# Attention, one turn in another order on all engines: six runs of score units for eight, the shared bank used twice in one turn, stack fills in the first turns

## The chip, the cores and the metric

The kernel runs on one core of a Trainium2 chip. The core has TensorE (PE in the profile; its weight loads are PEld), VectorE (DVE), ScalarE (ACT), GpSimd (POOL) and SyncE (SP), which here issues DMAs. The metric is the device time of one execution in microseconds (us), lower is better. Kernels are compared by the median of their runs.

## What is computed

Two transformer layers on x of 32 samples x 256 tokens x 128 features, in float32: a retention layer, a mixture of 16 experts, a full attention layer, and a layer that routes the best tokens of every sample. The change lies in the third, the attention:

```python
h = layernorm(x)
q = (h @ Wq.T + bq).reshape(b, s, 16, 8) * 8 ** -0.5     # b 32, s 256, 16 heads of 8
k = (h @ Wk.T + bk).reshape(b, s, 16, 8)
v = (h @ Wv.T + bv).reshape(b, s, 16, 8)
scores = einsum('bqhd,bkhd->bhqk', q, k)
out = einsum('bhqk,bkhd->bqhd', softmax(scores), v).reshape(b, s, 128)
x = x + out @ Wo.T + bo
```

## The kernel before, in words

Four phases run one after the other with a barrier between them. `attention_phase` goes through the 32 samples in a software pipeline. On each engine a list of steps with a lag is written out by hand, `pipeline(engine, [(step, lag), ...], B, B)`: in turn `it` (0, 1, 2, ...) the engine issues every step of the list in its order, each for sample `it - lag` where there is such a sample. So a list fixes the order of instructions on its engine, and a lag says how many turns after a sample's first step the step comes. The turns of two engines are tied together by semaphores alone: an instruction waits until what it reads is written and what it overwrites is read.

The steps of one sample, in the order of its data:

- `add_given` (GpSimd) adds the experts' result to x; `stats_of` and `moments` (VectorE), `inv_std` (GpSimd) and `norm` (ScalarE) make the layer norm. For samples 0 and 1 `moments_early` and `inv_std_early` stand at their own places.
- `transpose_h` (TensorE), `copy_hT` (ScalarE), `project_qk` and `project_v` (TensorE), `copy_qk` and `copy_v` (ScalarE).
- `split_qk(0)` and `split_qk(1)` (GpSimd) split k and q into a high and a low part; `store_k` and `store_q` (SyncE) write them to DRAM, and `fill_k` and `fill_q` read them back in another layout into `k_stack` and `q_stack`, which have three buffers. The stacks are set to 1.0 (k, by GpSimd) and 0.0 (q, by VectorE) once, before their first use; that takes three memsets each.
- The scores are made twice, in 8 units each of 4 matmuls (`scores`, L1511). A unit of kind "m" (`for_maximum(j)`, m0 to m7 below) has queries on the partitions, and VectorE reduces it over the keys (`maximum(j)`, L1374). `split_max` (GpSimd), `transpose_max` (TensorE), `copy_maxT` (ScalarE) and `give_max` (SyncE, two small DMAs for each half of the heads) put the maxima into rows of `q_stack`. A unit of kind "e" (`for_exponential(j)`, e0 to e7) has keys on the partitions and subtracts the maximum in the same matmul; ScalarE takes its exponential (`exponential(j)`, L1463), and `values(0)` to `values(3)` (TensorE, L1544) multiply two of them each with v. e0 waits for the maxima of half 0, e4 for those of half 1.
- `copy_o`, `by_token` (called "token" here), `normalise`, `transpose_o`, `copy_oT`, `output`, `add_y` end the attention of a sample; `stats3_of`, `moments3`, `inv_std3`, `norm3`, `weigh`, `add_up` and `store_out` prepare the next phase.

Units go into three PSUM slots of two banks; the table `UNITS` gives for each unit, in TensorE's order, kind, number, lag and slot, and before a unit TensorE waits until the unit that last had its slot has been read (`free_slot`). All else that goes through PSUM for a short time (v, oT, y, max0, max1, hT, token, qk) takes turns in one bank, `ps_misc`: `TURNS` lists the users in order, and each waits until the one before it has been read (`misc_free`). A score unit uses TensorE as two tiles of 64 rows, `values` as four tiles of 32 columns, and all other matmuls the whole array.

TensorE's list before has score units in eight runs, that is, with nothing else between them: m7 e7; m0; e0 m1; e1 m2; e2 m3 e3; m4; m5 e4 m6; e5 e6.

## Time and profile before

| | us |
|---|---|
| median of 3 runs (lowest to highest) | 1029.46 (1027.74 to 1031.27) |
| the profiled execution, its own time | 1028.35 |
| its span in the trace | 1026.6 |
| TensorE busy in the span | 909.6 (89%) |
| VectorE, ScalarE, GpSimd busy | 712.4, 637.1, 607.9 |

The time of an execution and its span differ by 1.75 us, which lies around the program. In the view of 40 slices attention takes slices 17 to 36. The chain that ended last covers only a tenth of the span and names the last phase alone, since each phase ends at a barrier; so what bounds attention has to be read from its own stretch: the busy time of the engines there, and the timeline of one turn. In a timeline a matmul's duration includes what it overlaps with the next, so lengths on TensorE are taken from start to start.

### The profile page before, as it was taken

How to read it: one execution, taken by the hardware profiler on the slowest of the kernel's cores; microseconds unless marked ns; L12 is line 12 of the kernel's file. 1: busy time of each engine (PE TensorE's matmuls, PEld its weight loads, DVE VectorE, ACT ScalarE, POOL GpSimd, SP SyncE). 2: the span in 40 equal slices, each digit the busy share in tenths (PEclk: the TensorE clock that was granted, in tenths of full speed). 3: DMA queues.
4: the chain of work that ended last, by engine and by line, in shares of the span. 5: the costliest groups of instructions: out<-in, count | busy, mean ns of one | idle time of the engine just before them, and what ended most of it. 6: DMA issues, size and time to landing. Idle time of an engine off the chain costs nothing. (4 is left out here: it accounts for less than half of the span.)

```text
span 1026.6 us, 28744 instructions
## 1 busy us (share of the span) xinstructions
PE 909.6 (89%) x10129; PEld 683.6 (67%) x10130; DVE 712.4 (69%) x1551; ACT 637.1 (62%) x1304; POOL 607.9 (59%) x1277
## 2 busy tenths in 40 slices
PE   6999999499989999169999999999999999944766
PEld 5888888279989999145666666666666666523654
DVE  4888888575544454347788888888888888826652
ACT  4777776322224444127888888888888888743552
POOL 4777776267737767544566676666676665344003
PEclk9999999699999999558999999999999999986998
DMA  8700000221123332134343545443444333202000
GB/s 310 294 3 2 3 2 2 80 76 54 50 69 95 91 92 78 59 124 146 115 146 111 152 127 157 127 130 124 134 147 137 120 123 116 68 17 68 3 3 21
DMA packets 66773, 96.88 MB, mean 94 GB/s; under 512 B 10706, under 2 KB 57426, under 8 KB 62162
## 3 DMA queue, kind: packets, MB, share of 16 engines
q1 hardware_dynamic: 61394, 84.00, 26.0%
q0 software_dynamic: 5248, 11.15, 3.2%
q8 instruction: 80, 1.31, 0.5%
q14 instruction: 51, 0.42, 0.1%
HBM read 57.60 MB, written 36.47 MB: 92 GB/s over the span
## 5 line engine op out<-in xcount | busy, mean ns | idle before, releaser
L1374 DVE TENSOR_REDUCE a_neg_max<-a_slot 128x4 f32<-128x1024 f32 x256 | 306.0, 1218 | 83.5 <-PE a_slot L1511 66.3
L1463 ACT ACTIVATE a_pT<-a_slot 128x1024 f32<-128x1024 f32 x256 | 255.5, 1026 | 8.9 <-PE a_slot L1511 5.2
L1544 PE MATMUL a_ps_o<-a_pT,a_v_pad 128*32 128x256 f32 x2048 | 137.9, 387 | 0.0
L1511 PE MATMUL a_slot<-a_k_stack,a_q_stack 62*128 62x256 f32 x1024 | 120.6, 316 | 4.2 <-DMA a_q_stack<-q_dram 2.4
L1511 PE MATMUL a_slot<-a_q_stack,a_k_stack 64*128 64x256 f32 x1024 | 114.5, 312 | 3.7 <-ACT a_pT L1463 1.9
L1511 PEld LDWEIGHTS a_slot<-a_k_stack,a_q_stack 62*128 62x128 f32 x1024 | 79.5, 191 | 46.7 <-issue 22.2
L727 POOL DMA_INDIRECT y_rows<-m_total,m_token x80 | 81.2, 1015 | 45.9 <-issue 32.9
L1511 PEld LDWEIGHTS a_slot<-a_q_stack,a_k_stack 64*128 64x128 f32 x1024 | 75.5, 187 | 34.9 <-issue 23.4
L331 DVE TENSOR_TENSOR r_score<-ps_score,r_decay 128x512 f32<-128x512 f32 x128 | 81.5, 678 | 7.9 <-PE ps_score L490 7.8
L1544 PEld LDWEIGHTS a_ps_o<-a_pT,a_v_pad 128*32 128x32 f32 x2048 | 53.6, 109 | 45.8 <-issue 19.4
L968 PE MATMUL m_banks<-m_xeT,m_w_pair 128*128 128x128 f32 x640 | 79.6, 278 | 0.0
L720 POOL DMA_INDIRECT sorted_in<-h,m_slot x64 | 63.9, 998 | 26.1 <-issue 18.6
L968 PEld LDWEIGHTS m_banks<-m_xeT,m_w_pair 128*128 128x128 f32 x640 | 76.1, 195 | 0.3 <-ACT m_xeT L878 0.3
L849 DVE COPY m_w_pair<-expert_up 128x512 f32 x80 | 31.2, 432 | 57.9 <-PE m_banks L968 57.3
L386 ACT ACTIVATE r_h<-x,r_shift,r_rstd 128x128 f32<-128x128 f32 x128 | 56.7, 497 | 12.2 <-POOL r_shift L258 11.7
L920 PE MATMUL m_banks<-h2T,shared_up 128*128 (+1 forms) x256 | 61.6, 385 | 2.5 <-DVE m_hidden L776 2.4
L870 ACT ACTIVATE m_gate<-m_banks 128x512 f32<-128x512 f32 x32 | 19.1, 597 | 66.7 <-PE m_banks L920 66.7
L885 ACT ACTIVATE m_gate_e<-m_banks 128x512 f32<-128x512 f32 x40 | 23.9, 597 | 57.6 <-PE m_banks L968 57.6
L1277 POOL TENSOR_TENSOR a_max_part<-a_neg_max,a_zeros 128x16 fp32r<-128x16 f32 x64 | 13.6, 212 | 70.6 <-DVE a_neg_max L1374 68.2
L1306 POOL TENSOR_TENSOR a_v_pad<-a_v_tok,a_zeros 128x128 f32<-128x128 f32 x64 | 24.2, 399 | 52.4 <-PE a_ps_o L1544 52.4
L920 PEld LDWEIGHTS m_banks<-h2T,shared_up 128*128 128x128 f32 x256 | 47.0, 193 | 9.0 <-issue 3.7
L1279 POOL TENSOR_TENSOR a_part<-a_qk,a_part 128x256 fp32r<-128x256 f32 x64 | 46.6, 727 | 5.0
(290 smaller groups left out, 2027.1 us busy)
## 6 DMA issues: line engine op xcount, KB each, us to landing
a_k_stack<-k_dram SPq DMA_DIRECT2D x64, 256.0 KB, 3.0
a_q_stack<-q_dram SPq DMA_DIRECT2D x64, 256.0 KB, 3.5
k_dram<-a_part SPq DMA_DIRECT2D x64, 128.0 KB
q_dram<-a_part SPq DMA_DIRECT2D x32, 256.0 KB
sorted_in<-h SPq DMA_DIRECT2D x10, 528.0 KB, 13.3
m_xe<-sorted_in SPq DMA_DIRECT2D x40, 132.0 KB
expert_up<-in_eu_dram SPq DMA_DIRECT2D x1, 4096.0 KB, 24.8
out_dram<-e_x_plus_h SPq DMA_DIRECT2D x32, 128.0 KB, 2.1
```

The source lines that it names most:

```text
L331: nc.vector.tensor_tensor(score[:, p, tile], ps_score[tile][:], own, ALU.mult).then_inc(score_done, 1)
L386: ins = nc.scalar.activation(h[:, p, t], x_sb[:, s * TPS + t, :], ACT.Identity, bias=shift[:, p, t:t + 1], scale=rstd[:, p, t:t + 1])
L720: nc.gpsimd.indirect_dma_start(sorted_in, bass.IndirectOffsetOnAxis(ap=slot[:, t:t + 1], axis=0), h2_all[:, t, :], None).then_inc(scattere ...
L727: nc.gpsimd.indirect_dma_start(y_rows, bass.IndirectOffsetOnAxis(ap=token[:, at:at + 1], axis=0), ye[:, t % RING, j], None).then_inc(store ...
L849: ins = nc.vector.tensor_copy(w_pair[:, p % 2, j], w_up[:, dve_experts[t][j]])
L920: ins = nc.tensor.matmul(bank[2 * which + p][:, f * S:(f + 1) * S], shared_up[:, which, f], h2T_all[:, bass.ds(s * S, S)], start=True, sto ...
L968: ins = nc.tensor.matmul(bank[PAIR * (p % 2) + j][:, f * P:(f + 1) * P], w_pair[:, p % 2, j, f * P:(f + 1) * P], xeT[:, p % 2, j], start=T ...
L1279: nc.gpsimd.tensor_tensor(low.bitcast(F32R), value, high, ALU.subtract).then_inc(steps, 1)
L1374: nc.vector.tensor_reduce(neg_max[:, p, half, t, :, g], slots[SLOT_OF["m", j]][:].rearrange("p (c r) s -> p c r s", c=TILES), AX.X, ALU.ma ...
L1463: nc.scalar.activation(pT[:, j % PT_RING], slots[SLOT_OF["e", j]][:], ACT.Exp).then_inc(e_read, 1)
L1511: ins = nc.tensor.matmul(slot[:, tile * UT + r], weights[at, n, half, g * UT + r, of_weights].bitcast(F32R), moving[at, n, half, g * UT + ...
L1544: ins = nc.tensor.matmul(ps_o[q * APAD:(q + 1) * APAD, g // 2], v_pad[:, p, t, g * UNIT + q], pT[:, (2 * g + t) % PT_RING, q], start=g % 2 ...
```

## The change

No arithmetic changes; every engine has the same instructions, in another order, with these differences in the code:

- TensorE's list and `UNITS`: m0 moves to the end of the list with lag 2, so that it stands directly ahead of e0 m1; m4 stands directly ahead of m5 e4; the 16 units stand in six runs, m0 e0 m1; m2 e1; e2 m3 e3; m4 m5 e4; e5 m6 e6; e7 m7. The slots are dealt out anew.
- `project_v` (lag 1 for 2) and `transpose_o` (lag 5 for 6) stand next to each other and share one turn of `ps_misc`: v in the first half of the bank, oT in the second (`MISC_SIDES`). `copy_v` waits in addition until the transposes that share its turn are done.
- The lists of ScalarE, VectorE, GpSimd and SyncE get another order and other lags.
- The memsets of the stacks move from ahead of the first turn into turns 3 to 5 on GpSimd (`preset_k_stack`) and 2 to 4 on VectorE (`preset_q_stack`).

On TensorE in the middle of the phase, `k_stack,q_stack` is a unit of kind m and `q_stack,k_stack` one of kind e, with its slot. Before, from v (L1601) over m7 e7, values(2), m0, oT (L1609), e0 m1, y (L1617) to e1 m2:

```order
L1601 MATMUL a_ps_misc<-a_wv,a_hT 128x128 x2
L1511 MATMUL a_slot0<-a_k_stack,a_q_stack 128x256 x4
L1511 MATMUL a_slot1<-a_q_stack,a_k_stack 128x256 x4
L1544 MATMUL a_ps_o<-a_pT,a_v_pad 32x256 x8
L1511 MATMUL a_slot2<-a_k_stack,a_q_stack 128x256 x4
L1609 MATMUL a_ps_misc<-ident,a_o_tok 128x128 x2
L1511 MATMUL a_slot1<-a_q_stack,a_k_stack 128x256 x4
L1511 MATMUL a_slot0<-a_k_stack,a_q_stack 128x256 x4
L1617 MATMUL a_ps_misc<-a_wo,a_oT 128x128 x2
L1511 MATMUL a_slot2<-a_q_stack,a_k_stack 128x256 x4
L1511 MATMUL a_slot1<-a_k_stack,a_q_stack 128x256 x4
```

m0 stands alone here, between values(2) and oT, and so does m4 later in the turn. Now, where the lines are v L1617, oT L1625, y L1633, values L1555:

```order
L1617 MATMUL a_ps_misc<-a_wv,a_hT 128x128 x2
L1625 MATMUL a_ps_misc<-ident,a_o_tok 128x128 x2
L1522 MATMUL a_slot1<-a_q_stack,a_k_stack 128x256 x4
L1522 MATMUL a_slot0<-a_k_stack,a_q_stack 128x256 x4
L1555 MATMUL a_ps_o<-a_pT,a_v_pad 32x256 x8
L1522 MATMUL a_slot2<-a_k_stack,a_q_stack 128x256 x4
L1522 MATMUL a_slot1<-a_q_stack,a_k_stack 128x256 x4
L1522 MATMUL a_slot0<-a_k_stack,a_q_stack 128x256 x4
L1633 MATMUL a_ps_misc<-a_wo,a_oT 128x128 x2
L1522 MATMUL a_slot1<-a_k_stack,a_q_stack 128x256 x4
L1522 MATMUL a_slot2<-a_q_stack,a_k_stack 128x256 x4
L1593 MATMUL a_ps_misc<-ident,a_max_part 16x128 x2
```

m0 has moved from between values(2) and oT to ahead of e0, and oT from there to directly behind v.

SyncE's queue in the middle of the phase, one turn, before:

```order
L1184 DMA a_k_stack<-k_dram 32x2048 x2
L1202 DMA a_q_stack<-a_max_T 2x4x256 x2
L1193 DMA a_q_stack<-q_dram 32x1x2048 x2
L1202 DMA a_q_stack<-a_max_T 2x4x256 x2
L1171 DMA k_dram<-a_part 16x8x256 x2
L1176 DMA q_dram<-a_part 128x2x256
L1211 DMA out_dram<-e_x_plus_h 128x2x128
```

Here each pair of transfers of maxima has a read back ahead of it. Now:

```order
L1196 DMA a_q_stack<-q_dram 32x1x2048 x2
L1205 DMA a_q_stack<-a_max_T 2x4x256 x2
L1187 DMA a_k_stack<-k_dram 32x2048 x2
L1205 DMA a_q_stack<-a_max_T 2x4x256 x2
L1174 DMA k_dram<-a_part 16x8x256 x2
L1179 DMA q_dram<-a_part 128x2x256
L1214 DMA out_dram<-e_x_plus_h 128x2x128
```

The read back of q stands ahead of both transfers of maxima and of the read back of k, and the stores of the next sample end the turn.

GpSimd at the start of the phase, before (`x<-x,h` is `add_given`, the four small ones `inv_std_early`):

```order
L1230 MEMSET a_k_stack 128x2048 x3
L1237 TENSOR_TENSOR x<-x,h 128x256 x2
L1251 TENSOR_TENSOR a_ve<-a_mv,a_eps 128x2
L1253 TENSOR_TENSOR a_minus_mean<-a_zeros,a_mv 128x2
L1257 TENSOR_TENSOR a_rstd<-a_ve,a_half_pow 128x2
L1259 TENSOR_TENSOR a_shift<-a_minus_mean,a_rstd 128x2
L1237 TENSOR_TENSOR x<-x,h 128x256
```

Here all three memsets stand ahead of the first addition. Now, up to the second memset:

```order
L1242 TENSOR_TENSOR x<-x,h 128x256 x2
L1256 TENSOR_TENSOR a_ve<-a_mv,a_eps 128x2
L1258 TENSOR_TENSOR a_minus_mean<-a_zeros,a_mv 128x2
L1262 TENSOR_TENSOR a_rstd<-a_ve,a_half_pow 128x2
L1264 TENSOR_TENSOR a_shift<-a_minus_mean,a_rstd 128x2
L1235 MEMSET a_k_stack 128x2048
L1242 TENSOR_TENSOR x<-x,h 128x256
L1256 TENSOR_TENSOR a_ve<-a_mv,a_eps 128x2
L1258 TENSOR_TENSOR a_minus_mean<-a_zeros,a_mv 128x2
L1262 TENSOR_TENSOR a_rstd<-a_ve,a_half_pow 128x2
L1264 TENSOR_TENSOR a_shift<-a_minus_mean,a_rstd 128x2
L1235 MEMSET a_k_stack 128x2048
```

The first two additions and the first layer norm stand ahead of the first memset; two memsets still stand ahead of the first `split_qk`, which comes behind the last row and one more `add_given`.

```diff
-UNITS = (("e", 6, 5, 2), ("m", 7, 4, 0), ("e", 7, 5, 1), ("m", 0, 3, 2), ("e", 0, 4, 1), ("m", 1, 3, 0),
...
+UNITS = (("e", 0, 4, 1), ("m", 1, 3, 0), ("m", 2, 3, 1), ("e", 1, 4, 2), ("e", 2, 4, 0), ("m", 3, 3, 2), ("e", 3, 4, 1),
+         ("m", 4, 3, 2), ("m", 5, 3, 0), ("e", 4, 4, 1), ("e", 5, 4, 1), ("m", 6, 3, 0), ("e", 6, 4, 2), ("e", 7, 4, 1),
+         ("m", 7, 3, 0), ("m", 0, 2, 2))
+MISC_SIDES = {"v": (0,), "oT": (1,), "y": (0,), "max1": (0,),
+              "hT": (0,), "token": (0, 1), "qk": (0, 1), "max0": (0,)}
...
+        misc = {name: ps_misc[:, sides[0] * S:(sides[-1] + 1) * S] for name, sides in MISC_SIDES.items()}
...
-            pipeline(sp, [(store_k, 3), (store_q, 3), (store_out, 9), (fill_k, 3), (give_max(1), 5), (fill_q, 3), (give_max(0), 4),
+            pipeline(sp, [(fill_q, 4), (give_max(1), 6), (fill_k, 4), (give_max(0), 5), (store_k, 3), (store_q, 3), (store_out, 10),
...
-            for n in range(BUFS):
-                nc.gpsimd.memset(k_stack[:, n], 1.0).then_inc(preset_k, 1)
+
+            def preset_k_stack(s, p, r):
+                if s < BUFS:
+                    nc.gpsimd.memset(k_stack[:, s], 1.0).then_inc(preset_k, 1)
...
-            pipeline(pool, [(split_max(0), 5), (weigh, 9), (add_given, 0), (inv_std_early, 1), (split_qk(0), 3), (inv_std, 2),
-                            (split_max(1), 5), (split_qk(1), 3), (bias, 5), (pad_v, 4), (inv_std3, 8)], B, B)
+            pipeline(pool, [(weigh, 12), (pad_v, 7), (add_given, 2), (inv_std_early, 3), (split_qk(0), 5), (split_qk(1), 5),
+                            (inv_std3, 10), (split_max(1), 7), (bias, 6), (split_max(0), 6), (inv_std, 3), (preset_k_stack, 3)], B, B)
...
-            pipeline(dve, [(given_added, 0), (maximum(0), 4), (add_up, 9), (add_y, 7), (maximum(1), 4),
-                           (maximum(2), 4), (moments3, 8), (stats_of, 0), (y_is_added, 7), (maximum(3), 4),
-                           (normalise, 6), (maximum(4), 4), (moments, 1), (stats3_of, 7), (maximum(5), 4),
-                           (settle3, 7), (maximum(6), 4), (settle, 0), (moments_early, 0), (maximum(7), 4),
-                           (preset_v_pad, 2)], B, B)
+            pipeline(dve, [(stats_of, 1), (settle_early, 1), (moments_early, 1), (maximum(6), 5), (settle3, 8), (moments3, 8),
+                           (add_up, 10), (settle, 1), (moments, 1), (maximum(7), 5), (maximum(0), 4), (add_y, 7),
+                           (maximum(1), 4), (maximum(2), 4), (y_is_added, 7), (stats3_of, 7), (maximum(3), 4),
+                           (normalise, 6), (maximum(4), 4), (maximum(5), 4), (given_added, 0), (preset_q_stack, 2),
+                           (preset_v_pad, 3)], B, B)
...
             def copy_v(s, p, r):
                 after(act, v_done, s + 1)
+                after_most(act, oT_done, s - 4 + 1, B)
...
-            pipeline(act, [(copy_qk, 1), (exponential(4), 4), (copy_maxT(0), 3), (copy_o(0), 4),
-                           (exponential(5), 4), (exponential(6), 4), (copy_v, 1), (exponential(7), 4),
-                           (copy_oT, 5), (exponential(0), 3), (norm, 0), (copy_maxT(1), 3), (exponential(1), 3),
-                           (copy_o(1), 4), (copy_hT, 0), (exponential(2), 3), (exponential(3), 3),
-                           (norm3, 6)], B, B)
+            pipeline(act, [(copy_maxT(0), 3), (exponential(5), 4), (exponential(6), 4), (exponential(7), 4), (copy_oT, 5), (copy_v, 1),
+                           (exponential(0), 3), (norm, 0), (exponential(1), 3), (copy_maxT(1), 3), (copy_hT, 0),
+                           (copy_o(1), 4), (exponential(2), 3), (exponential(3), 3), (norm3, 7), (exponential(4), 3),
+                           (copy_qk, 0), (copy_o(0), 3)], B, B)
...
-            TURNS = (("v", 2, v_copied, 1, 0), ("oT", 6, oT_copied, 1, 0), ("y", 6, y_added, 1, 0),
...
+            TURNS = ((("y", 6, y_added, 1, 0),), (("max1", 4, maxT_copied, 2, 1),), (("hT", 1, hT_copied, 1, 0),),
+                     (("token", 5, otok_copied, 1, 0),), (("qk", 1, qk_copied, 1, 0),), (("max0", 3, maxT_copied, 2, 0),),
+                     (("v", 1, v_copied, 1, 0), ("oT", 5, oT_copied, 1, 0),))
...
-            pipeline(pe, [(for_exponential(6), 5), (project_v, 2), (for_maximum(7), 4), (for_exponential(7), 5),
-                          (values(2), 5), (for_maximum(0), 3), (transpose_o, 6), (for_exponential(0), 4),
-                          (for_maximum(1), 3), (output, 6), (for_exponential(1), 4), (for_maximum(2), 3),
...
+            pipeline(pe, [(for_exponential(0), 4), (for_maximum(1), 3), (output, 6), (for_maximum(2), 3), (for_exponential(1), 4),
                           (transpose_max(1), 4), (values(3), 5), (transpose_h, 1), (for_exponential(2), 4),
-                          (for_maximum(3), 3), (for_exponential(3), 4), (by_token, 5), (values(0), 4),
...
+                          (for_maximum(3), 3), (for_exponential(3), 4), (by_token, 5), (values(0), 4), (for_maximum(4), 3),
+                          (for_maximum(5), 3), (for_exponential(4), 4), (project_qk, 1), (values(1), 4),
+                          (transpose_max(0), 3), (for_exponential(5), 4), (for_maximum(6), 3), (for_exponential(6), 4),
+                          (project_v, 1), (transpose_o, 5), (for_exponential(7), 4), (for_maximum(7), 3), (values(2), 4),
+                          (for_maximum(0), 2)], B, B)
```

## Rows read from the trace of the kernel before

**Rows 1.** The page of the profile, its first line.
```profile
span 1026.6 us, 28744 instructions
```

**Rows 2.** Stretches: us; busy (count) of PE, PEld, DVE, ACT, POOL; PEclk; DMA, GB/s.
```profile
450.50:470.00 19.50, 17.20 (x96) 11.06 (x96) 14.86 (x18) 7.24 (x13) 8.45 (x22) 0.50 0.46 154
...
491.17:883.09 391.92, 387.88 (x4250) 246.63 (x4246) 328.87 (x547) 337.13 (x581) 256.16 (x598) 1.00 0.43 132
```

**Rows 3.** Timeline, TensorE: start, duration, engine, line, operation; m0, samples 3 and 31.
```profile
491.17 0.50 PE L1511 MATMUL a_slot<-a_k_stack,a_q_stack 62*128 62x256 f32 x4
...
883.09 0.50 PE L1511 MATMUL a_slot<-a_k_stack,a_q_stack 62*128 62x256 f32 x4
```

**Rows 4.** Timeline, TensorE, parts of one turn.
```profile
645.25 0.51 PE L1511 MATMUL a_slot<-a_k_stack,a_q_stack 62*128 62x256 f32 x4
645.68 0.44 PE L1609 MATMUL a_ps_misc<-ident,a_o_tok 128*128 128x128 f32 x2
646.06 0.51 PE L1511 MATMUL a_slot<-a_q_stack,a_k_stack 64*128 64x256 f32 x4
...
649.80 0.50 PE L1511 MATMUL a_slot<-a_q_stack,a_k_stack 64*128 64x256 f32 x4
650.14 0.40 PE L1511 MATMUL a_slot<-a_k_stack,a_q_stack 62*128 62x256 f32 x4
650.38 0.41 PE L1511 MATMUL a_slot<-a_q_stack,a_k_stack 64*128 64x256 f32 x4
650.73 0.66 PE L1588 MATMUL a_ps_misc<-ident,a_oT_pad 128*128 128x128 f32 x4
651.31 1.07 PE L1544 MATMUL a_ps_o<-a_pT,a_v_pad 128*32 128x256 f32 x16
...
654.38 0.40 PE L1511 MATMUL a_slot<-a_k_stack,a_q_stack 62*128 62x256 f32 x4
654.89 0.38 PE L1577 MATMUL a_ps_misc<-ident,a_max_part 128*16 128x128 f32 x2
```

**Rows 5.** Timeline, ScalarE, the same turn.
```profile
646.60 1.03 ACT L1463 ACTIVATE a_pT<-a_slot 128x1024 f32<-128x1024 f32 x1
...
654.29 0.47 ACT L1448 ACTIVATE a_qk<-a_ps_misc,a_bk 128x256 f32<-128x256 f32 x1
```

**Rows 6.** Timeline, SyncE's queue and TensorE; in brackets idle time and its releaser.
```profile
873.63 1.16 SPq L1184 DMA_DIRECT2D a_k_stack<-k_dram  x2
874.83 1.44 SPq L1202 DMA_DIRECT2D a_q_stack<-a_max_T  x2
...
877.75 0.50 PE L1511 MATMUL a_slot<-a_q_stack,a_k_stack 64*128 64x256 f32 x4 [0.56 <-DMA a_q_stack<-a_max_T]
```

**Rows 7.** Timeline of the first turns, GpSimd, VectorE, SyncE's queue, TensorE.
```profile
426.08 5.29 POOL L1230 MEMSET a_k_stack<- 128x2048 f32 x3
...
430.64 1.76 DVE L1329 MEMSET a_q_stack<- 128x2048 f32 x1 [0.38 <-issue]
...
433.37 0.20 POOL L1251 TENSOR_TENSOR a_ve<-a_mv,a_eps 128x2 f32<-128x2 f32 x1 [0.63 <-DVE a_mv L1358]
...
434.75 0.73 POOL L1237 TENSOR_TENSOR x<-x,h 128x256 f32<-128x256 f32 x1
...
440.07 0.61 POOL L1277 TENSOR_TENSOR a_part<-a_qk,a_zeros 128x256 fp32r<-128x256 f32 x1 [2.55 <-ACT a_qk L1448]
...
445.88 1.21 SPq L1193 DMA_DIRECT2D a_q_stack<-q_dram  x2
...
450.50 1.65 PE L1511 MATMUL a_slot<-a_k_stack,a_q_stack 62*128 62x256 f32 x12 [2.44 <-DMA a_q_stack<-q_dram]
```

**Rows 8.** Timeline of the last turns, VectorE.
```profile
915.08 0.45 DVE L1401 BATCH_NORM_STATS2 e_stats<-x 128x6 f32<-128x128 f32 x2
...
918.45 0.42 DVE L1413 TENSOR_REDUCE w_tok<-e_product 128x2 f32<-128x256 f32 x1 [2.92 <-POOL e_product L1317]
918.79 0.24 DVE L1408 BATCH_NORM_AGGREGATE e_mv<-e_stats 128x2 f32<-128x6 f32 x2
```

More of the change, by code:

```diff
@@ L1454, in step @@
                         after(act, max_in[(s - 1) % BUFS][half], 16 * TILES * ((s - 1) // BUFS + 1))
-                    nc.scalar.copy(max_T[:, half], ps_misc[0:PARTS * HH, 0:S]).then_inc(maxT_copied, 1)
+                    nc.scalar.copy(max_T[:, half], misc[f"max{half}"][0:PARTS * HH]).then_inc(maxT_copied, 1)
                 return step
@@ L1548, in values @@
                 return step
[L1551 to L1553 removed]
+            TURNS = ((("y", 6, y_added, 1, 0),), (("max1", 4, maxT_copied, 2, 1),), (("hT", 1, hT_copied, 1, 0),),
+                     (("token", 5, otok_copied, 1, 0),), (("qk", 1, qk_copied, 1, 0),), (("max0", 3, maxT_copied, 2, 0),),
+                     (("v", 1, v_copied, 1, 0), ("oT", 5, oT_copied, 1, 0),))
             def misc_free(name, s):
[L1556 to L1562 removed]
+                at = [name in [user[0] for user in turn] for turn in TURNS].index(True)
+                lags = {user[0]: user[1] for user in TURNS[at]}
+                it = s + lags[name]
+                first = TURNS[at][0][0]
+                if name != first and 0 <= it - lags[first] < B:
+                    return
+                for back in range(1, 4 * len(TURNS)):
+                    it_then = it - (back - at + len(TURNS) - 1) // len(TURNS)
+                    users = [user for user in TURNS[(at - back) % len(TURNS)] if 0 <= it_then - user[1] < B]
+                    for _, lag, read, per, which in users:
+                        after(pe, read, per * (it_then - lag) + which + 1)
+                    if users:
                         return
```

39 lines of the change are left out of this document (15 added, 24 removed).

## The prediction

> **What bounds the kernel now.** I read the stretches first, then the list of TensorE from one unit to the next. m0 of sample 3 starts at 491.17 and m0 of sample 31 at 883.09 [rows 3]: 28 turns in 391.92 us, 14.00 each. In them TensorE is busy for 387.88 us, 99%, at a granted clock of 1.00 (2.4 GHz); ScalarE is busy for 337, VectorE for 329, GpSimd for 256 [rows 2], which is 12.0, 11.7 and 9.1 us a turn. So in these 28 turns, 38% of the span [rows 1], a turn lasts as long as TensorE's list, and a shorter list shortens it until another engine, some 2 us behind, has a wait that TensorE sees. Before 491 the pipeline fills, after 883 it drains; there nothing is full, and chains through all engines count.
>
> A busy share doesn't say whether the list could be shorter; starts do. In the run e2 m3 e3 the units start at 649.80, 650.14 and 650.38, and the next group at 650.73 [rows 4]: 0.34, 0.24 and 0.35 us. A unit in the middle of a run costs 0.24. m0, alone in its run, takes from 645.25 to 645.68, 0.43. So each run costs about 0.19 us beside its units, however many they are. Whole-array groups behave alike: the two transposes of o take 0.38 (645.68 to 646.06), the four of token 0.58 (650.73 to 651.31), so two more in an open group cost 0.20, and opening one 0.18.
>
> **The change, TensorE's list.** The 16 units and all other groups stay; three openings go.
> - Six runs for eight, m0 and m4 no longer alone: 2 x 0.19 = -0.38 us a turn.
> - v and oT next to each other: -0.18. No row shows two different whole-array groups side by side with different operands; the bounds are 0 and -0.20, and I take the value of the token group, the nearest thing.
> - max0 starts 0.51 after m6 (654.38 to 654.89), where the group behind e3 starts after 0.35: its turn in the shared bank has to wait for ScalarE's second activation of qk, which ends at 654.76 [rows 5]. Now a group of values, 1.07 long [rows 4], lies between qk and max0, and the wait goes: -0.10 (0 to -0.16).
>
> Sum: -0.66, a list of 13.34 us.
>
> **Waits that the new order makes.** I lay the other engines beside this list, from m0 = 0: e0 at 0.34, m1 at 0.58, y at 0.91, m2 at 1.55, max1 at 2.3, hT at 3.6, e4 at about 7.1. A slot is free for its next unit at least 0.2 us early for 15 of the 16 units. The exception is m2: it takes the slot of e0, with only m1 and y in between. e0 ends at 0.58, its exponential takes 1.03 [rows 5], so the slot is free at about 1.7 and m2 waits 0.15; e1, max1 and all the rest queue behind it. From there the chain runs e1, its exponential, the copy of max1 (behind it on ScalarE), hT: another 0.05. Together +0.2 (0 to 0.4). A turn then lasts 13.54, 0.46 less; over 28 turns -12.9 us. Bounds: all savings and no wait, -0.66 x 28 = -18.5; the two runs alone and the waits at 0.2, -0.18 x 28 = -5.0.
>
> The added wait in `copy_v` (for the transposes of o) stands on ScalarE ahead of e0's exponential, which TensorE's m2 needs. v and oT end at about 11.7 of the turn, while ScalarE reaches the two copies only behind e7's exponential, near 13.0: it costs nothing as long as ScalarE is that late; if it were earlier it would wait with nothing urgent behind it.
>
> **SyncE's queue.** The maxima of half 1 now go out behind `fill_q`, and e4 waits for them. Their copy ends near 3.8 and e4 is due near 7.3 with the waits above: 3.5 us. From the issue of such a pair right behind `fill_k` (873.63, then 874.83) to the matmul that waited for it (877.75) it took 2.9 us [rows 6]: 0.6 in hand. `fill_q` itself waits for the store of q, which GpSimd's split ends at about the start of the turn, and has to be issued (1.21 us [rows 7]) by 3.8: that is close, and is the rival below. The first `fill_q` needed 4.6 us from its issue (445.88) to the matmul that waited for it (450.50) [rows 7]. The Trainium skill (DMA: Bandwidth & Descriptors, Queues, rings and completion order) says that each DMA engine consumes descriptors in ring order; by that the maxima would land only behind the whole `fill_q`, 4.6 - 1.2 = 3.4 us after their own issue, an estimate. No run here shows the two in this order; the sum would be the same, with 0.1 us in hand for 0.6.
>
> **The start.** GpSimd's three memsets take 5.29 us from 426.08, and only then x is added [rows 7]. The first `split_qk` starts at 440.07, and from it follow the store, the read back and m0 of sample 0 at 450.50. In the new order GpSimd does two additions (0.70 each), waits for the moments, does `inv_std_early` (1.4: 433.37 to 434.75), a memset (1.76, as on VectorE), an addition, `inv_std_early`, a memset, an addition: VectorE had the moments 0.97 after its last memset (430.64 + 1.76, then 433.37); without memsets it can start at about 426.9, behind the bias matmul, so I take 428.0 for the moments, and 428.0 + 2 x (1.4 + 1.76 + 0.7) = 435.7. The split waits for ScalarE's copy of qk as well, which came 5.3 after `inv_std_early` (434.75 to 440.07): now 429.4 + 5.3 = 434.7, earlier. So the first split starts at 435.7, 4.3 us sooner, not 5.3, since two of the three memsets still lie ahead of it. VectorE's memsets (1.76 each) move behind the first moments and are done long before `fill_q`. `fill_q` now goes first and waits for the later store; about even. I take -4.3 for the fill (-2 to -6: in 450 to 470 TensorE runs at 0.50, 1.2 GHz [rows 2], and when it rises isn't set by the order alone; all of that stretch at full clock would be worth some 8 us, a rise a few us later costs half of those).
>
> **The end.** The last sample's `stats3_of` is at 915.08, yet its `moments3` only at 918.79, behind `add_up` of the sample before at 918.45 [rows 8]: in VectorE's list `add_up` of an older sample stands ahead. In the new list `add_up` comes two turns later than `moments3`, and on GpSimd `weigh` of the sample before comes behind `inv_std3` of the last. The last moments can start at 915.6: -3.2 us (0 to -3.3).
>
> Sum: -12.9 - 4.3 - 3.2 = -20.4. The profiled execution took 1028.35, which gives 1008.0; the median of the runs lies 1.1 above it, so 1009. By the bounds: -27.8 to -7.0, that is 1002 to 1022.
>
> **Rivals.**
> - *Another engine becomes the bound.* ScalarE is busy 12.0 us of what would be 13.5, in fixed order, with VectorE at 11.7. If its copies (ahead of hT, token, max0) come late by 0.25 us more, a turn lasts 13.8: -5.6 - 7.5 = -13.1, 1016.
> - *The change doesn't shorten the list*: what a run costs is not in its opening, and returns at other borders. Turns stay at 14.0 and the two ends alone bring -7.5: 1022. Against it stand the two lengths of a unit, 0.43 and 0.24.
> - *Slower: the maxima come late.* The place is `fill_q` ahead of `give_max(1)`. If the store of q lands late, `fill_q` holds SyncE's queue, the maxima go out late, and e4 and all behind it wait in every turn, us for us. The 0.6 in hand go first; a turn is back at 14.0 when they are 1.06 late, and the kernel is slower when the waits also eat the 7.5 of the ends (0.27 a turn), that is from 1.33 on. Two us late gives 13.54 + 1.4 = 14.9: +26 - 7.5, 1048. For it: GpSimd's list, 9.1 us long, starts each turn's chain with a wait for VectorE's m3 and ends it with the split of q. Against: a late e4 delays the next m3 too, from which that chain starts, so part of a delay is paid back.
>
> **How the numbers follow.** My forecast (1002 to 1013) has a chance of 0.58, another engine 0.16, a list that isn't shorter 0.12, late maxima 0.14. About 0.3%, 3 us, is what a measurement of this kernel can tell from no change. Faster by more: the first two, and 0.08 of the third (the ends have to bring over 3 us), 0.82. Slower by more: 0.10 of the late maxima. Between: 0.04 of each of the last two, 0.08. The range is that of the bounds, 1002 to 1022; it leaves out the late maxima and half of the third case, 0.2.
>
> **What would show it.** Right: PE from m0 to m0 near 13.5 us; m5 starting 0.34 after m4; oT about 0.65 behind the start of v and 0.2 long; a small wait at m2 for ScalarE; the first split near 435.7; the last moments right behind the last stats. Wrong: waits at e4 or e0 for the maxima, a turn of 13.8 with idle time ahead of hT or token, or m0 of sample 0 later than 448.

## The result and the profile after

The changed kernel takes 1025.88 us (median of 15 runs, 1022.93 to 1029.41) and the kernel before 1031.27 (15 runs, 1027.74 to 1033.88). The ratio is 0.9948, 95% interval 0.9934 to 0.9962: some 5.4 us faster. The forecast was 1009 with a range of 1002 to 1022, so the sign was right and the size wrong by a factor of four: -20.4 forecast, -5.4 measured. The profiled execution of the changed kernel took 1027.74 (span 1026.0), 1.9 above its median; that of before, 1028.35, lies 2.9 below the median of its 15 runs. So the two traces differ by 0.6 only, and the other 4.8 us lie between profiled executions and medians.

One cut through both traces serves for all that follows: GpSimd's first instruction in attention, the starts of y (`output`) of sample 0, of sample 27 and of sample 31 (y(0), y(27), y(31) below), and the start of the routed layer behind attention. Columns of the order of time: start, time, engine, line, operation, out<-in, count, idle time before. Before:

```profile
425.86 0.10 POOL L1225 MEMSET a_half_pow<- 128x2 f32 x1 [7.84 <-POOLq L97]
...
492.65 0.60 PE L1617 MATMUL a_ps_misc<-a_wo,a_oT 128*128 128x128 f32 x3
870.88 0.71 PE L1617 MATMUL a_ps_misc<-a_wo,a_oT 128*128 128x128 f32 x4
913.60 0.88 PE L1617 MATMUL a_ps_misc<-a_wo,a_oT 128*128 128x128 f32 x4 [0.55 <-ACT a_oT L1476]
926.07 0.59 PE L2162 MATMUL d_ps<-ident,w_tok 128*32 128x128 f32 x2 [11.59 <-PEq L97]
```

After:

```profile
426.71 0.10 POOL L1228 MEMSET a_half_pow<- 128x2 f32 x1 [7.84 <-POOLq L97]
...
492.71 0.71 PE L1633 MATMUL a_ps_misc<-a_wo,a_oT 128*128 128x128 f32 x4
872.96 0.71 PE L1633 MATMUL a_ps_misc<-a_wo,a_oT 128*128 128x128 f32 x4
913.85 0.68 PE L1633 MATMUL a_ps_misc<-a_wo,a_oT 128*128 128x128 f32 x4 [0.55 <-ACT a_oT L1488]
923.42 0.59 PE L2177 MATMUL d_ps<-ident,w_tok 128*32 128x128 f32 x2 [8.88 <-PEq L97]
```

| stage of the trace, us | before | after | change | forecast |
|---|---|---|---|---|
| up to the start of attention | 425.86 | 426.71 | +0.85 | 0 |
| start of attention to y(0) | 66.79 | 66.00 | -0.79 | -4.3 |
| 27 turns, y(0) to y(27) | 378.23 | 380.25 | +2.02 | -12.4 |
| y(27) to y(31), pipeline running empty | 42.72 | 40.89 | -1.83 | -0.5 |
| y(31) to the routed layer | 12.47 | 9.57 | -2.90 | -3.2 |
| routed layer to the end | 100.53 | 102.58 | +2.05 | 0 |
| span | 1026.6 | 1026.0 | -0.6 | -20.4 |

The phases ahead of attention and the routed layer behind it hold code that isn't touched; in all twelve traces attention starts between 425.29 and 426.82. Without those two stages the traces differ by 3.5 us, nearer to the 5.4 of the medians.

The 27 turns hold two things that must be kept apart. By the starts of y, 17 of them last 13.75 to 13.79 us, where before all lasted 14.00 to 14.02: the list did get shorter, by 0.25 a turn, 6.8 us in all. The other ten are longer: 27 x 13.755 is 371.4, and 380.25 were taken, 8.9 more. The longest, from y of sample 19 to that of sample 20, takes 17.42. The stretch that answers to [rows 2] (columns: stretch, length, busy time and count of PE, PEld, DVE, ACT, POOL, then PE's granted clock, DMA share, GB/s) has TensorE busy for 374.64 of 391.20 us, 96% and no longer 99%:

```profile
491.80:883.00 391.20, 374.64 (x4226) 240.10 (x4222) 330.95 (x543) 338.95 (x577) 249.38 (x592) 1.00 0.44 132
```

**A turn without disturbance.** TensorE, one undisturbed turn of after, the places that the forecast spoke of (`k_stack,q_stack` is a unit m, `q_stack,k_stack` a unit e):

```profile
645.31 0.40 PE L1522 MATMUL a_slot<-a_q_stack,a_k_stack 64*128 64x256 f32 x4
...
645.88 0.71 PE L1633 MATMUL a_ps_misc<-a_wo,a_oT 128*128 128x128 f32 x4
646.83 0.51 PE L1522 MATMUL a_slot<-a_k_stack,a_q_stack 62*128 62x256 f32 x4 [0.24 <-ACT a_pT L1475]
647.82 1.07 PE L1555 MATMUL a_ps_o<-a_pT,a_v_pad 128*32 128x256 f32 x16
649.02 0.41 PE L1585 MATMUL a_ps_misc<-ident,a_h 128*128 128x128 f32 x2
...
656.14 0.71 PE L1617 MATMUL a_ps_misc<-a_wv,a_hT 128*128 128x128 f32 x4
656.69 0.38 PE L1625 MATMUL a_ps_misc<-ident,a_o_tok 128*128 128x128 f32 x2
657.00 0.50 PE L1522 MATMUL a_slot<-a_q_stack,a_k_stack 64*128 64x256 f32 x4
```

and ScalarE at the same place:

```profile
645.75 1.02 ACT L1475 ACTIVATE a_pT<-a_slot 128x1024 f32<-128x1024 f32 x1 [0.33 <-PE a_slot L1522]
...
647.61 1.02 ACT L1475 ACTIVATE a_pT<-a_slot 128x1024 f32<-128x1024 f32 x1
648.53 0.35 ACT L1467 COPY a_max_T<-a_ps_misc 16x256 f32<-16x256 f32 x1
```

v and oT together take 0.86 (656.14 to 657.00). y took 0.64 up to the next unit before (646.73 to 647.37); now m2 starts 0.95 behind it, a wait of 0.31: e0 is at its end only at 645.71 (0.40 after its start), its exponential runs from 645.75 to 646.77, and then its slot is free. hT starts 1.20 behind the start of the values group, where another of the same turn is followed after 1.00 (651.86, behind 650.86): 0.20 of waiting for the copy of max1 (648.53 to 648.88), which stands behind e1's exponential.

**The late maxima.** From the waits between 500 and 872 (who waited for whom, us in total, times, the longest): SyncE for landings before, then SyncE and TensorE after:

```profile
SPq L47 <- DMA k_dram<-a_part: 0.3, 1, 0.3
```

```profile
SPq L47 <- DMA q_dram<-a_part: 34.6, 26, 3.6
...
PE a_slot L1522 <- DMA a_q_stack<-a_max_T: 5.0, 7, 2.0
```

Before, SyncE had next to no wait for a landing. After, it waits in 26 turns for the store of q to land, 1.3 us on average and up to 3.6. The longest turn shows what comes of it, on SyncE and TensorE in the order of time, and in the granted clock of two stretches:

```profile
757.95 0.54 SPq L1179 DMA_DIRECT2D q_dram<-a_part  x1
...
762.66 1.20 SPq L1196 DMA_DIRECT2D a_q_stack<-q_dram  x2
763.91 1.42 SPq L1205 DMA_DIRECT2D a_q_stack<-a_max_T  x2
...
764.71 0.74 PE L1522 MATMUL a_slot<-a_k_stack,a_q_stack 62*128 62x256 f32 x8
767.39 0.50 PE L1522 MATMUL a_slot<-a_q_stack,a_k_stack 64*128 64x256 f32 x4 [1.95 <-DMA a_q_stack<-a_max_T]
...
769.28 1.93 PE L1555 MATMUL a_ps_o<-a_pT,a_v_pad 128*32 128x256 f32 x16
```

```profile
764.00:767.00 3.00, 1.44 (x24) 0.74 (x16) 2.66 (x5) 1.56 (x3) 2.47 (x8) 1.00 0.78 216
769.00:771.00 2.00, 2.00 (x17) 0.59 (x16) 0.00 (x0) 0.84 (x2) 0.62 (x2) 0.50 0.00 0
```

Here the store of q is issued at 757.95, `fill_q` only at 762.66, and the maxima of half 1 behind it at 763.91, 2.2 us later in the turn than in an undisturbed one (5.19 behind y for 3.03). e4, which could have followed m5, waits 1.95. Then the granted clock falls to 0.50 (1.2 GHz), and the next values group takes 1.93 for 1.07: with the wait of 1.95 the turn is 3.66 longer than an undisturbed one.

The ten long turns don't have one cause. In five the maxima went out later than 3.03 behind y: in y(19) since the store of q landed 4.65 us after its issue, where the others took 2.3 to 3.1; in y(15) and y(3) since that store was itself issued 1.4 and 0.3 later, in y(15) behind a store of k whose issue took 2.02 for 0.6; in y(10) and y(22) since the issue of `fill_q`'s second transfer took 1.72 and 1.61 for 0.59. In the other five they went out on time and landed late. Their landing is taken from the events in the trace of the semaphore that e4 waits for: in the 17 undisturbed turns 2.7 to 3.3 us after their issue, which is 0.1 to 0.8 ahead of e4, 0.5 on average; in those five turns 3.5 to 4.5 us.

**The fill.** GpSimd's first split, TensorE's m0 m1 m2 and later m4 m5 of sample 0, and VectorE's maxima of sample 0 with what lies between them:

```profile
436.25 0.61 POOL L1282 TENSOR_TENSOR a_part<-a_qk,a_zeros 128x256 fp32r<-128x256 f32 x1
447.77 1.65 PE L1522 MATMUL a_slot<-a_k_stack,a_q_stack 62*128 62x256 f32 x12 [4.41 <-DMA a_k_stack<-k_dram]
453.28 1.22 PE L1522 MATMUL a_slot<-a_k_stack,a_q_stack 62*128 62x256 f32 x8 [2.51 <-DVE a_neg_max L1385]
...
454.12 2.36 DVE L1385 TENSOR_REDUCE a_neg_max<-a_slot 128x4 f32<-128x1024 f32 x2 [0.89 <-PE a_slot L1522]
456.86 1.76 DVE L1339 MEMSET a_q_stack<- 128x2048 f32 x1 [0.38 <-issue]
458.78 0.91 DVE L1344 MEMSET a_v_pad<- 128x1024 f32 x1 [0.16 <-issue]
460.16 1.21 DVE L1385 TENSOR_REDUCE a_neg_max<-a_slot 128x4 f32<-128x1024 f32 x1
```

m0 of sample 0 comes 2.7 us sooner (450.50 before [rows 7]), 3.6 counted from the start of attention. But two of VectorE's fills, 2.67 us together, lie between the maxima of m5 and m6, and m4 stands in the slot of m3, so TensorE waits 2.51 us for that maximum. By y of sample 0 only 0.8 is left. TensorE's granted clock, too, rises from 0.50 to 1.00 no sooner: at 470.2 before and at 471.5 after, 44.3 and 44.8 into attention.

**The end.** The last sample's statistics and moments on VectorE:

```profile
915.10 0.49 DVE L1412 BATCH_NORM_STATS2 e_stats<-x 128x6 f32<-128x128 f32 x2
915.62 0.25 DVE L1419 BATCH_NORM_AGGREGATE e_mv<-e_stats 128x2 f32<-128x6 f32 x2
```

They follow each other at once, 3.2 us sooner than the moments of [rows 8]; the routed layer starts 2.65 sooner.

**The routed layer**, whose code isn't touched, takes 2.05 us more in this execution. The same eight matmuls there, before and after:

```profile
945.34 1.99 PE L2193 MATMUL d_ps<-d_wqkv,d_xnT 128*128 128x256 f32 x8 [0.78 <-ACT d_xnT L2041]
```

```profile
942.93 3.46 PE L2208 MATMUL d_ps<-d_wqkv,d_xnT 128*128 128x256 f32 x8 [0.78 <-ACT d_xnT L2056]
```

The granted clock is 1.00 during them before and 0.57 after; over the whole layer it is 0.86 and 0.83. In the ten traces of the experiments, all with the same code there, the layer takes 98.5 to 102.0 us, at 0.88 in the shortest. The 102.58 of after lies just beyond these; I take the 2 us for that scatter and not for an effect of the change.

### The profile page after: what moved, and what is told of

It is laid out like the page before. It is cut to its first block and busy times, and to the rows that moved or that the text cites. A ratio compares the mean times of both kernels' runs of the same rounds, so it can differ in the third digit from the quotient of the medians.

```text
span 1026.0 us, 28626 instructions
## 1 busy us (share of the span) xinstructions
PE 900.1 (88%) x10130; PEld 681.0 (66%) x10130; DVE 717.0 (70%) x1551; ACT 642.5 (63%) x1304; POOL 603.9 (59%) x1277
## 5 line engine op out<-in xcount | busy, mean ns | idle before, releaser
L1475 ACT ACTIVATE a_pT<-a_slot 128x1024 f32<-128x1024 f32 x256 | 252.3, 1028 | 39.4 <-PE a_slot L1522 34.8
L1555 PE MATMUL a_ps_o<-a_pT,a_v_pad 128*32 128x256 f32 x2048 | 138.8, 389 | 0.0
L1522 PE MATMUL a_slot<-a_k_stack,a_q_stack 62*128 62x256 f32 x1024 | 111.9, 309 | 17.2 <-ACT a_pT L1475 7.9
L1522 PEld LDWEIGHTS a_slot<-a_q_stack,a_k_stack 64*128 64x128 f32 x1024 | 78.7, 188 | 29.3 <-issue 13.2
L1555 PEld LDWEIGHTS a_ps_o<-a_pT,a_v_pad 128*32 128x32 f32 x2048 | 53.8, 110 | 49.5 <-issue 22.4
L386 ACT ACTIVATE r_h<-x,r_shift,r_rstd 128x128 f32<-128x128 f32 x128 | 56.7, 496 | 12.4 <-POOL r_shift L258 11.9
L256 POOL TENSOR_TENSOR r_rstd<-r_ve,r_half 128x2 f32<-128x2 f32 x64 | 45.3, 707 | 5.0
```

The source lines that it names most:

```text
L256: nc.gpsimd.tensor_tensor(rstd[:, p], ve[:], half[:], ALU.pow).then_inc(rstd_done, 1)
L386: ins = nc.scalar.activation(h[:, p, t], x_sb[:, s * TPS + t, :], ACT.Identity, bias=shift[:, p, t:t + 1], scale=rstd[:, p, t:t + 1])
L1475: nc.scalar.activation(pT[:, j % PT_RING], slots[SLOT_OF["e", j]][:], ACT.Exp).then_inc(e_read, 1)
L1522: ins = nc.tensor.matmul(slot[:, tile * UT + r], weights[at, n, half, g * UT + r, of_weights].bitcast(F32R), moving[at, n, half, g * UT + ...
L1555: ins = nc.tensor.matmul(ps_o[q * APAD:(q + 1) * APAD, g // 2], v_pad[:, p, t, g * UNIT + q], pT[:, (2 * g + t) % PT_RING, q], start=g % 2 ...
```

## The experiments

The theory was: three separate things took the gain, namely the late maxima (8.9 us), the waits of the new order (0.51 a turn where 0.2 was forecast) and the moved fills with the slot of m4 (about 3 us). The rivals were transfers that are late whatever the order, ScalarE as the bound, and the low clock up to 470, by which nothing sooner would help. "y(0)" below is the start of the first y, "in attention" the same counted from attention's own start in that trace, which is what an edit inside attention can change. "min turn" is the shortest from y to y in the 27 turns, "excess" is what the 27 turns take beyond an undisturbed one each.

| kernel | median us (runs) | ratio to before, 95% | y(0) | in attention | min turn | excess |
|---|---|---|---|---|---|---|
| before | see above | 1 | 492.65 | 66.79 | 14.00 | 0.2 |
| after | 1025.88 (15) | 0.9948 (0.9934 to 0.9962) | 492.71 | 66.00 | 13.75 | 8.9 |
| max1_first | 1017.85 (4) | 0.9867 (0.9846 to 0.9888) | 492.38 | 65.85 | 13.74 | 0.2 |
| fillk_first | 1016.17 (4) | 0.9864 (0.9845 to 0.9883) | 491.61 | 65.78 | 13.75 | 0.3 |
| copy1_early | 1019.04 (4) | 0.9879 (0.9856 to 0.9902) | 492.20 | 65.64 | 13.57 | 8.3 |
| presets_only | 1026.08 (6) | 0.9946 (0.9928 to 0.9963) | 489.70 | 62.88 | 14.01 | 0.2 |
| slots45 | 1018.82 (1) | one run | 491.25 | 65.33 | 13.75 | 6.2 |
| presets_early | 1022.07 (5) | 0.9916 (0.9897 to 0.9935) | 491.22 | 65.03 | 13.74 | 9.2 |
| all_four | 1009.91 (5) | 0.9805 (0.9788 to 0.9821) | 490.50 | 64.63 | 13.58 | 0.4 |
| all_four_split | 1039.19 (6) | 1.0083 (1.0069 to 1.0097) | 489.31 | 63.94 | 14.68 | 0.3 |
| all_four_split2 | 1010.69 (5) | 0.9791 (0.9772 to 0.9810) | 487.05 | 61.75 | 13.69 | 0.1 |
| all_four_e0 | 1010.51 (5) | 0.9792 (0.9768 to 0.9816) | 491.47 | 65.00 | 13.60 | 0.2 |

**The maxima ahead of `fill_q`.**

```diff
-pipeline(sp, [(fill_q, 4), (give_max(1), 6), (fill_k, 4), ...
+pipeline(sp, [(give_max(1), 6), (fill_q, 4), (fill_k, 4), ...
```

> The changed kernel with one edit on SyncE: the maxima of half 1 go out ahead of fill_q again. Theory, late maxima: in the changed kernel fill_q follows the store of q at once and waits for its landing (34.6 us in 26 waits), the maxima of half 1 stand behind it, and ten turns last longer than 13.76, 8.9 us in all. Then without fill_q in front every turn lasts 13.76, TensorE has no wait at e4 for the maxima, and the kernel takes 9 us less than the changed one, near 1017 (1014 to 1020). Rival, slow landings: the transfers are late in some turns whatever stands ahead of them in the queue; then waits at e4 or at m0 add up to 5 us or more again and the time stays near 1026.

It came out as the theory says: 1017.85, 8.0 less than after. All 27 turns last 13.74 to 13.77, and in them no view of waits names the maxima's transfer or the store of q any more. With nothing ahead of them the maxima land 2.6 to 3.3 us after their issue. What stays on TensorE is m2's wait:

```profile
PE a_slot L1522 <- ACT a_pT L1475: 6.5, 27, 0.2
```

**`fill_k` ahead of the maxima.**

```diff
-pipeline(sp, [(fill_q, 4), (give_max(1), 6), (fill_k, 4), ...
+pipeline(sp, [(fill_k, 4), (give_max(1), 6), (fill_q, 4), ...
```

> The changed kernel with fill_k ahead of the maxima of half 1 and fill_q behind them, as in the kernel before, at the new lags. What stands ahead of the maxima is again 512 KB of stack fill, but its source, the store of k, was issued 1.3 us sooner than that of q. Theory A, the queue is held: the maxima are late because SyncE waits for the landing of the store of q; then nearly all excess over 13.76 goes (under 1 us in 27 turns, 9.0 in the changed kernel) and the time is 1017 to 1019. Theory B, transfer behind transfer: the maxima are late since their own transfer lies behind the fill's; then the turns in which they went out on time and landed late (2.6 of the 9.0 us) stay, 2 us or more of excess, 1019 to 1022.

1016.17 and an excess of 0.3: by what was expected, theory A. SyncE still waits for a landing, but for the store of k, which was issued sooner, 0.6 us a time:

```profile
SPq L47 <- DMA k_dram<-a_part: 13.8, 23, 1.1
```

The test is less clean than it was meant to be: `fill_k` goes out 1.9 to 2.4 us ahead of the maxima, where `fill_q` in after mostly led by 1.2 to 1.8. So it doesn't rule out theory B. That the place behind `fill_q` cost the 9 us is shown by the two runs; how much of it is the held queue and how much transfer behind transfer is read from after's own turns: in five of the ten long ones the maxima went out later than 3.03 behind y (6.0 of the 8.9 us), in the other five they went out on time and were late all the same. The landings bear out both: here the maxima land 2.7 to 3.3 us after their issue, closely behind `fill_q` in after 2.7 to 4.5, and in before, 1.2 behind `fill_k`, 2.7 to 4.1.

**The copy of max1 ahead of e1's exponential.**

```diff
-... (norm, 0), (exponential(1), 3), (copy_maxT(1), 3), (copy_hT, 0),
+... (norm, 0), (copy_maxT(1), 3), (exponential(1), 3), (copy_hT, 0),
```

> The changed kernel with one edit on ScalarE: the copy of max1 stands ahead of e1's exponential. Theory, waits of the new order: hT starts 1.20 us behind the values group instead of 1.00, since its turn in the shared bank waits for the copy of max1, which stands behind a 1.02 us exponential. With the copy first the wait goes, a turn lasts 13.55 for 13.75 (28 x 0.2 = 5.6 us), and the maxima go out 0.35 us sooner, which takes some of the late ones away: 1014 to 1020. Rival, ScalarE is the bound: the 0.35 us come back at e1's exponential and show as a wait at m3 or at the values groups; turns stay at 13.75 and the time near 1026.

The values group and hT, and further on e4 in the turn of y 672.50:

```profile
647.19 1.07 PE L1555 MATMUL a_ps_o<-a_pT,a_v_pad 128*32 128x256 f32 x16
648.19 0.44 PE L1585 MATMUL a_ps_misc<-ident,a_h 128*128 128x128 f32 x2
...
680.18 0.50 PE L1522 MATMUL a_slot<-a_q_stack,a_k_stack 64*128 64x256 f32 x4 [1.14 <-DMA a_q_stack<-a_max_T]
```

hT follows after 1.00, and an undisturbed turn lasts 13.58, so ScalarE isn't the bound. The side effect that was expected didn't come: the excess stays at 8.3. The maxima do go out sooner in most turns, from 2.5 behind y on, directly behind `fill_q`'s issue; but they land 2.9 to 4.8 us after their issue, and e4 is due 0.17 sooner.

**The fills alone, in the old order.** Only the memsets of the stacks move, into the first turns of the kernel before.

```diff
-            for n in range(BUFS):
-                nc.gpsimd.memset(k_stack[:, n], 1.0).then_inc(preset_k, 1)
+            def preset_k_stack(s, p, r):
+                if s < BUFS:
+                    nc.gpsimd.memset(k_stack[:, s], 1.0).then_inc(preset_k, 1)
...
+   ... (inv_std3, 8), (preset_k_stack, 1)], B, B)
```

> The kernel before with one part of the change alone: GpSimd's and VectorE's stack fills are done in the first turns. Theory, the order of the units eats the fill's gain: in the changed kernel m0 of sample 0 starts 2.7 us sooner but the first y at the same time, since m4 takes the slot that m3 has just filled and TensorE waits 2.5 us for its maximum. In the old order of units the gain then stays: m0 of sample 0 near 447, the first y near 489.7 for 492.65, and the kernel 3 us faster than before. Rival, the clock: TensorE runs at half clock until about 470 in both, and what comes sooner only waits for that; the first y stays near 492.6 and the time at that of before.

```profile
447.33 1.65 PE L1515 MATMUL a_slot<-a_k_stack,a_q_stack 62*128 62x256 f32 x12 [3.86 <-DMA a_q_stack<-q_dram]
```

The first y comes 2.95 us sooner as expected, though attention starts 0.96 later in this trace; in attention the gain is 3.9. So the low clock doesn't take it: the granted clock itself rises sooner, at 467.6 for 470.2. How much of the 3.9 is the order and how much the earlier rise isn't separated. The other stages are those of before within 0.8. The median fell by 5.5 us, 1.6 more than the fill gives; the traces don't show where that is.

**The slots of m4 and m5 exchanged.**

```diff
-         ("m", 4, 3, 2), ("m", 5, 3, 0), ("e", 4, 4, 1), ...
+         ("m", 4, 3, 0), ("m", 5, 3, 2), ("e", 4, 4, 1), ...
```

> The changed kernel with the slots of m4 and m5 exchanged, so that m4 no longer follows m3 in the same slot. Theory, order of the units: the wait of 2.5 us ahead of m4 of sample 0 goes; VectorE had 0.9 us of idle time there, so the maxima of sample 0 end 0.9 us sooner and so does the first y, near 491.8; the turns stay at 13.75. Rival, the clock: the first y stays at 492.7, whatever TensorE waits for before 470.

The first y comes at 491.25, 1.46 sooner than after, but 0.8 of this lies ahead of attention; in attention it is 0.7 (0.9 expected). The time of this one run is too low for that edit: its routed layer took 98.5 us, the shortest of all, and its excess was 6.2. No verdict on the time follows from it.

**VectorE's fills one turn sooner.**

```diff
-   (given_added, 0), (preset_q_stack, 2), (preset_v_pad, 3)], B, B)
+   (given_added, 0), (preset_q_stack, 1), (preset_v_pad, 2)], B, B)
```

> The changed kernel with VectorE's stack fills one turn sooner (lags 1 and 2 for 2 and 3). Theory, the moved fills stand in the way: in the changed kernel the third fill of q_stack (1.76 us, 456.86) and the fill of v_pad (0.91, 458.78) lie between the maxima m5 and m6 of sample 0, so the maximum of m6 starts at 460.16, 3 us after m5's, and m7 and all behind wait for it. One turn sooner they lie in VectorE's idle time ahead of 448.6; m6's maximum then starts near 457.5, the first y near 489.9 for 492.71, and the kernel takes 3 us less than the changed one: 1023. Rival, the clock: whatever comes sooner before 470 waits for the full clock; the first y stays near 492.5 and the time near 1026.

```profile
458.18 1.23 DVE L1385 TENSOR_REDUCE a_neg_max<-a_slot 128x4 f32<-128x1024 f32 x1 [2.01 <-PE a_slot L1522]
```

The fills are gone from between the maxima, but two thirds of their 3 us return as VectorE's wait of 2.01 for m6, which TensorE reaches only behind max0 and the copies of qk. In attention the first y is 1.0 us sooner (some 3 were expected), and the median is 3.8 less than after; the traces don't show the rest.

**The four edits together.**

> The changed kernel with four edits together: the maxima of half 1 ahead of fill_q, the copy of max1 ahead of e1's exponential, VectorE's stack fills one turn sooner, the slots of m4 and m5 exchanged. If the three causes (late maxima 9 us, the wait at hT 0.17 a turn, the fill 3 us) are separate, they add up: turns of 13.58 without excess, the first y near 489.5, and 1010 (1007 to 1013). Rival, one bound behind the other: SyncE's chain of stores, fills and maxima is full, and the shorter turn brings late transfers back; then turns vary again or stay at 13.75 and the time is 1014 or more.

The edits are the four shown above (max1_first, copy1_early, slots45, presets_early). 1009.91: this beats both kernels. The turns are 13.58 with an excess of 0.4, and the causes nearly add up; the two edits of the fill bring 1.4 in attention together, and 0.7 and 1.0 alone, less than the 3 that were expected.

**One run more.** Two tries, the second with ScalarE's list adjusted to the first one's edit:

```diff
-   (for_maximum(4), 3), (for_maximum(5), 3), (for_exponential(4), 4), (project_qk, 1), (values(1), 4),
+   (for_maximum(4), 3), (project_qk, 1), (for_maximum(5), 3), (for_exponential(4), 4), (values(1), 4),
...
-   (norm3, 7), (exponential(4), 3), (copy_qk, 0), (copy_o(0), 3)], B, B)
+   (norm3, 7), (copy_qk, 0), (exponential(4), 3), (copy_o(0), 3)], B, B)
```

> The kernel with the four edits, with one run of score units more: the projection of q and k stands between m4 and m5, so that m4 is alone in its run, as in the kernel before. Theory, a run has a price of its own of 0.19 us: a turn lasts 0.19 longer (13.77 for 13.58), less up to 0.09 since the wait of max0 for the copy of qk goes; 2.8 to 5.3 us more than the four edits alone. Rival, the price is not in the opening: the turn stays within 0.03 of that of the four edits, and the time within 1 us.

> The kernel with the four edits and one run of score units more: the projection of q and k stands between m4 and m5 on TensorE, and, other than in the last try, ScalarE's copy of qk stands ahead of e4's exponential, so that the copy isn't 0.94 us late for max0. Theory, a run has a price of its own: 0.19 us, less the 0.09 that max0 waited for the copy: turns of 13.68 for 13.58, 2.8 us more than 1009.9. Rival, no price of its own: turns within 0.03 of 13.58 less the 0.09, 13.5, and 1 to 3 us less than 1009.9.

The first lasts 14.70 a turn and shows another thing: ScalarE's copy of qk stood behind e4's exponential, e4 now came behind qk, and max0 waited for the copy:

```profile
646.40 0.38 PE L1593 MATMUL a_ps_misc<-ident,a_max_part 128*16 128x128 f32 x2 [0.94 <-ACT a_qk L1460]
```

14.70 - 0.94 = 13.76 was what the theory had forecast. In the second, turns last 13.70 (13.68 expected; 13.5 without a price for a run):

```profile
643.67 0.50 PE L1522 MATMUL a_slot<-a_k_stack,a_q_stack 62*128 62x256 f32 x4
644.11 0.70 PE L1610 MATMUL a_ps_misc<-a_hT,a_wq 128*128 128x256 f32 x2
...
645.83 1.07 PE L1555 MATMUL a_ps_o<-a_pT,a_v_pad 128*32 128x256 f32 x16
646.84 0.39 PE L1593 MATMUL a_ps_misc<-ident,a_max_part 128*16 128x128 f32 x2
```

m4 alone takes 0.44, and max0 follows its values group after 1.01, without a wait. So a run has its price; the first y at 487.05 gives it back, 2.9 us sooner in attention than with the four edits alone, and the median is theirs within 0.8. In the fill the copies of qk are over sooner, and the granted clock rises at 465.2 for 470.3; the two weren't separated.

**e0 ahead of m0.**

```diff
-UNITS = (("e", 0, 4, 1), ("m", 1, 3, 0), ... ("m", 7, 3, 0), ("m", 0, 2, 2))
+UNITS = (("e", 0, 4, 1), ("m", 0, 3, 2), ("m", 1, 3, 0), ... ("m", 7, 3, 0))
...
-pipeline(pe, [(for_exponential(0), 4), (for_maximum(1), 3), ... (for_maximum(0), 2)], B, B)
+pipeline(pe, [(for_exponential(0), 4), (for_maximum(0), 3), (for_maximum(1), 3), ...], B, B)
```

> The kernel with the four edits, and e0 ahead of m0 in their run: m0 goes from the first to the second place, with its slot as before. m2 takes e0's slot and waits 0.31 us for e0's exponential. Theory A, that wait is one of place: e0 ends 0.34 sooner, its exponential too (ScalarE idles 0.34 ahead of it), m2's wait goes and a turn lasts 13.3 (13.25 to 13.4), 6 to 9 us less than 1009.9. Theory B, the three slots are full there: m0 ends 0.3 later, its maximum, the addition of y and the maxima of m1 and m2 come later on VectorE, and the wait moves to e1, which takes m0's slot, or to max1, which waits for the addition of y: turns of 13.5 to 13.7, the time within 3 us of 1009.9.

```profile
654.85 0.71 PE L1633 MATMUL a_ps_misc<-a_wo,a_oT 128*128 128x128 f32 x4
655.55 0.50 PE L1522 MATMUL a_slot<-a_k_stack,a_q_stack 62*128 62x256 f32 x4
656.00 0.50 PE L1522 MATMUL a_slot<-a_q_stack,a_k_stack 64*128 64x256 f32 x4
656.44 0.39 PE L1593 MATMUL a_ps_misc<-ident,a_max_part 128*16 128x128 f32 x2
```

Theory B. m2's wait is nearly gone (0.70 behind y), but e1 comes 0.45 behind m2 and max1 0.44 behind e1 where it was 0.34 and 0.33 in after, and e0, whose weight loads wait for the maxima's transfer (11.6 us in 27 turns), comes 1.05 behind its values group for 1.00. Turns stay at 13.60: the wait has moved, as theory B said for full slots; what each of the three places waits for isn't shown one by one.

## Why the prediction was wrong

- **The price of a run held.** m4 directly ahead of m5, v and oT next to each other came as forecast. By the starts, the runs of units take 5.04 us a turn for 5.55 (0.16 of waiting for the copy of qk left out), v and oT 0.86 for 1.02, max0's wait is 0.09 for 0.16, and a few other groups give 0.02: the list is 0.76 shorter, forecast 0.66. The second try with one run more confirms the price from the other side.
- **The new waits were sized too small,** 0.51 a turn and not 0.2 (0.31 at m2, 0.20 at hT). The chain e0, exponential, m2 was the right one. The step that failed is "e0 ends at 0.58": that adds the 0.24 at which the next unit can start, but e0 ends 0.40 after its start. The spacing of starts on a pipelined engine is a price; for who waits for the result the length counts. For hT I added 0.05 for a copy that stands behind a whole exponential of 1.02. With both errors, and the list 0.1 shorter, a turn is 13.75 and not 13.54: 0.21 x 27 = 5.7 us. Part of it was open to repair, as the copy's edit shows (13.58).
- **The late maxima were priced at nothing.** The step that failed is "0.6 in hand", taken for the same in every turn, by which the sum gave them no time, though the rival "the maxima come late" named the place and the mechanism. As a typical value 0.6 was fair: 0.1 to 0.8 is in hand in the undisturbed turns. The sum had no term for what differs from turn to turn by more than that, and a landing later than e4 is due is paid in full: 8.9 us. Two things differ. One is when the maxima go out: `fill_q` now follows `store_q` with only `store_out` between, so SyncE's queue holds a landing and the issue of a fill ahead of them each turn, where before [rows 6] `fill_k` and the maxima lay in between; each of these was late at times (6.0 us). The other is how long they take to land closely behind a fill, 2.7 to 4.5 us. The rival's picture, late in every turn by the same amount, was wrong too: ten turns of 27 are longer, by 0.1 to 3.66 us. The Trainium skill (DMA: Bandwidth & Descriptors, Queues, rings and completion order) has each DMA engine take descriptors in ring order; the forecast worked out from it 3.4 us to the landing, behind the whole `fill_q`, with 0.1 in hand, and kept 0.6 for the sum. The trace agrees in part: the maxima land later behind a fill than alone, but not behind the whole of it. In the turn from y(1) e4 had them at 6.55 behind y without a wait, and the last of `fill_q` landed not before 7.08.
- **The fill's gain came and went.** The first split started at 436.25 (435.7 forecast), counted from the start of attention 4.7 us sooner than before, so that step held. m0 of sample 0 came at 447.77 (446.2), 3.6 sooner in attention: 1.1 went since `fill_q` waits for the store that was issued last (441.48, 1.9 behind its end). At the first y 0.8 was left. The step that failed is "VectorE's memsets (1.76 each) move behind the first moments and are done long before `fill_q`": of three only the first two are; the third and that of v_pad lay between the maxima of sample 0. And the slots were laid out for the full turn, where e units stand between m units; in the first turn m4 directly follows m3 in its slot. The two edits against this bring 1.4 of the 3.5 that are missing; the cause of the rest stays open between the later copies of qk and the clock, which rises as late as before (all_four_split2, with both sooner, is 2.9 faster there).
- **The end held:** -2.90 from the last y to the routed layer, -3.2 forecast. The emptying pipeline gave 1.8, where the sum has 0.5 for these turns. The end's edit wasn't undone alone: that the gain comes from the new order is read from VectorE's rows and not tested.
- **The base.** The forecast stood on a median of three runs, 1029.46; of fifteen it is 1031.27. That made the forecast 1.8 us too low and is no fault of a step.

In the profiled execution 5.7 (waits), 8.9 (late maxima), 3.5 (fill), 0.85 (attention starts later) and 2.05 (clock in the routed layer), less about 1 by which both ends together were better than forecast, lead from -20.4 to -0.6 (20.0 against 19.8, the rest is rounding). With the late maxima and part of the others repaired, all_four takes 1009.91, where the forecast had seen the changed kernel. That it is the same number is luck: against before its trace has 11.2 from the turns where 12.4 was forecast, 2.2 from the fill for 4.3, and 5.7 from both ends for 3.7.
